# State-space layer between two batches: a new order of the work, other PSUM banks, tanh in place of silu in the gated MLP, and copies, skip terms and first scalings put on VectorE and GpSimd

## The reference

```python
def _mamba(h, in_proj_W, conv_w, conv_b, x_proj_W, dt_proj_W, dt_proj_b, A_log, Dp, out_proj_W):
    x, z = jnp.split(h @ in_proj_W, 2, axis=-1)          # 512 channels each
    x = _silu(causal_conv4(x, conv_w) + conv_b)          # 4 taps, per channel
    xdbl = x @ x_proj_W                                  # 16 + 32 + 32 columns
    dt = jax.nn.softplus(xdbl[..., :16] @ dt_proj_W + dt_proj_b)
    Bm, Cm = xdbl[..., 16:48], xdbl[..., 48:]
    A = -jnp.exp(A_log)
    # for every time step: hst = hst * exp(dt*A) + dt*B*x ;  y = sum_n hst * C
    _, ys = jax.lax.scan(step, h0, seq)
    y = ys + Dp * x                                      # the skip term
    return y * _silu(z) @ out_proj_W

h = _ln(x, norm1_w, norm1_b) * (1 + s1) + sh1
x = x + g1 * (_mamba(h) + flip(_mamba(flip(h))))
h = _ln(x, norm2_w, norm2_b) * (1 + s2) + sh2
x = x + g2 * (_silu(h @ w1) * (h @ w2) @ w3)
```

## Time and profile before

| | |
|---|---|
| median of 3 runs | 5845.14 us |
| profiled execution, its own time | 5844.69 us |
| its span | 5842.8 us |
| the fourth layer's pace | 8 batches of 128 units, one every 344.0 us |
| busy over the span: PE, DVE, ACT, POOL | 94%, 74%, 70%, 48% |
| instructions with a scan (L2480) | 1024, 2267 ns each |

### The profile page before, as it was taken

How to read it: one execution, slowest core, us unless ns; L and a number is a source line. 1 busy time by engine, 2 the same in 40 slices (tenths; PEclk the granted TensorE clock), 3 DMA queues, 4 the chain that set the end, 5 groups by cost and what they waited for, 6 DMA issues and landing times. The chain is left out here.

```text
span 5842.8 us, 74727 instructions
## 1 busy us (share of the span) xinstructions
PE 5511.4 (94%) x27336; PEld 2865.9 (49%) x27336; DVE 4311.1 (74%) x5020; ACT 4113.3 (70%) x6785; POOL 2804.3 (48%) x2191
## 2 busy tenths in 40 slices
PE   8999999999999997999998999999999999999998
PEld 5444445555555554444444444444544445454445
DVE  6767744444444444776867989899898999989898
ACT  3555454554444543555558989899998989989897
POOL 0000012232222321010106969699696978969697
PEclk8999999999999998999999999999999999999999
DMA  5342420000000004233223020110202012020200
GB/s 145 47 66 34 83 30 3 1 3 3 2 3 1 3 2 63 48 62 63 48 45 69 30 54 30 42 43 24 59 30 54 30 29 56 26 58 30 54 30 22
DMA packets 171934, 222.33 MB, mean 38 GB/s; under 512 B 40881, under 2 KB 107274, under 8 KB 171314
## 3 DMA queue, kind: packets, MB, share of 16 engines
q1 hardware_dynamic: 171570, 217.56, 17.1%
HBM read 152.90 MB, written 30.49 MB: 31 GB/s over the span
## 5 line engine op out<-in xcount | busy, mean ns | idle before, releaser
L2480 DVE TENSOR_TENSOR_SCAN l__h<-l__decay,psum 128x1024 f32<-128x1024 f32 x1024 | 2249.6, 2267 | 55.9 <-ACT l__decay L1928 15.5
L2446 POOL TENSOR_TENSOR l__hc<-l__h,l__c_rep 128x1024 f32<-128x1024 f32 x1016 | 2012.4, 2013 | 92.5 <-DMA l__c_rep<-l__c_dram 46.5
L1928 ACT ACTIVATE l__decay<-l__dt_rep,l__a_neg 128x511 f32<-128x511 f32 x2048 | 1339.6, 708 | 9.6 <-DVE l__h L2480 9.3
L1938 PEld LDWEIGHTS psum<-ident,l__dtx_B 128*128 128x128 f32 x8192 | 882.7, 141 | 850.9 <-DVE l__h L2480 496.1
L2564 PE MATMUL psum<-l__hc,l__gather 128*64 128x512 f32 x4096 | 1105.2, 618 | 139.8 <-POOL l__hc L2446 139.3
L1938 PE MATMUL psum<-ident,l__dtx_B 128*128 128x128 f32 x8192 | 1119.3, 280 | 35.6 <-DVE l__h L2480 16.8
L1912 ACT ACTIVATE l__dtx_B<-l__dtx_T,l__b_T 128x512 f32<-128x512 f32 x1664 | 1103.4, 709 | 5.5 <-PE psum L1938 3.4
L683 DVE TENSOR_REDUCE l__row_max<-psum 128x1 f32<-128x512 f32 x1024 | 648.7, 680 | 207.4 <-PE psum L717 203.8
L1367 POOL TENSOR_SCALAR l__probs<-l__probs,l__rec 128x512 f32<-128x512 f32 x512 | 348.6, 694 | 886.4 <-DVE l__rec L1363 886.4
L199 POOL TENSOR_SCALAR l__ln_var_eps<-l__ln_mean_var 128x4 f32<-128x4 f32 x56 | 16.1, 287 | 1433.6 <-DVE l__ln_mean_var L185 1433.6
L1040 ACT ACTIVATE l__probs<-psum 128x1024 f32<-128x1024 f32 x512 | 501.9, 1023 | 147.5 <-PE psum L1101 141.2
(11 more groups left out here) (184 smaller groups left out, 6193.9 us busy)
## 6 DMA issues: line engine op xcount, KB each, us to landing
l__c_rep<-l__c_dram SPq DMA_DIRECT2D x512, 128.0 KB, 2.8
l__dt_rep<-l__dt SPq DMA_DIRECT2D x128, 256.0 KB, 5.0
l__parts_dram<-l__parts SPq DMA_DIRECT2D x64, 384.0 KB, 3.5
l__q_stack<-l__parts_dram SPq DMA_DIRECT2D x192, 128.0 KB, 6.5
l__k_stack<-l__parts_dram SPq DMA_DIRECT2D x192, 128.0 KB, 9.1
l__w<-in_l_w SPq DMA_DIRECT2D x6, 1024.0 KB, 6.3
l__gate_rows<-l__gates_dram SPq DMA_DIRECT2D x24, 256.0 KB, 3.2
in_mod_w<-in_mod_w SPq DMA_DIRECT2D x1, 4608.0 KB, 17.8
```

The lines of the kernel that those rows point to most:

```text
L1928: nc.scalar.activation(decay[:, i % DECAYS, s, 1:T], dt_rep[:, w, c, s, 1:T], ACT.Exp, scale=a_neg[:, g, c, s:s + 1]).then_inc(S["decay"], 1)
L1938: last = nc.tensor.transpose(bx_psum(i)[:, s, t * P:(t + 1) * P], dtx_B[:, (k + 1) % 2, t, 2 * c + s, :, :].rearrange("p j d -> p (j d)"), ...
L2446: nc.gpsimd.tensor_tensor(hc[:, i % HCS, :, :], h[:, i % HS, :, :], c_of(i), ALU.mult).then_inc(S["hc"], 1)
L2480: nc.vector.tensor_tensor_scan(both(h[:, i % HS, :, :]), both(decay[:, i % DECAYS, :, :]), both(bx_psum(i)), 0.0, ALU.mult, ALU.add).then_ ...
```

## The change

- **VectorE.** The first chunk of the convolution comes between gates 1 and 2. The normalised rows (L193) follow the statistics at once. New on it are: the copy of the backward half of `dc`, the copy of the transposed B, the scaling and shift of the MLP's input out of PSUM (two), the four backward copies of dt*x transposed, four of the eight first scalings, and a second multiplication for each of the MLP's three products. The skip terms have gone.
- **GpSimd.** It makes the skip terms, eight instructions of 128 x 512 (`skip_terms`): xs forward + xs backward, then times D.
- **ScalarE.** Skip terms, half the copies, B's copy, the MLP's input and four scalings have gone; silu of x comes ahead of silu of z; the MLP uses tanh(u/2), from which VectorE makes u*(1 + tanh(u/2)) and then 0.5 times this times the second projection; the third tanh stands behind the first two units' decays.
- **TensorE.** The transposes of the next batch's layer norm come ahead of the last but two `y_sum`, the input projection begins in banks 0 and 1 between the last `y_sum`s, z's four projections come in one piece ahead of `project_x`, and the transposes of dt*x alternate between banks 4, 5 and 2, 3 in place of 0 and 1.
- **SyncE.** One wait for both halves of `dc` in place of two.

```diff
@@ -1843,9 +1845,10 @@
-        IN_BANKS = (2, 3, 0, 1)
+        IN_BANKS = (0, 1, 2, 3)
-        dt_banks = lambda c: psum[:, (2, 0, 4, 2)[c]:(2, 0, 4, 2)[c] + 2, :]
+        dt_banks = lambda c: psum[:, (0, 4, 2, 0)[c]:(0, 4, 2, 0)[c] + 2, :]
+        dtxT_bank = lambda c, w: bank[(4, 2)[c % 2] + w]
...
+        def scale_first(dve):
+            w, g, _ = split(0)
+            for op in range(VEC_OPS):
+                t, j = op // NJ, op % NJ
+                nc.vector.tensor_scalar(dtx_B[:, 1, t, :, j, :], dtx_T[:, w, t, :].rearrange("p (b d) -> p b d", d=HB),
+                                        b_T[:, w, t, NJ * g + j:NJ * g + j + 1], None,
+                                        ALU.mult).then_inc(S["dtxB_vec"], 1)
...
@@ between_gpsimd
+            if begin:
+                skip_terms(pool, end)
             if end:
                 norm.gpsimd(nc, pool, 1 if begin else 0)
...
+        def skip_terms(pool, end):
...
+            for c in range(IC):
+                pool.wait_ge(*S.at("xs", 2 * (c + 1)))
+                nc.gpsimd.tensor_tensor(y[:, c, :], xs[:, c, 0, :], xs[:, c, 1, ::-1], ALU.add).then_inc(S["y_first"], 1)
+                pool.wait_ge(*S.at("y_first", c + 1))
+                nc.gpsimd.tensor_scalar(y[:, c, :], y[:, c, :], dp[:, c:c + 1], 1.0, ALU.mult, ALU.mult)\
+                    .then_inc(S["y_init"], 1)
...
@@ between_vector
+            if begin and end:
+                gate(0)
+                gate(1)
+                convolve(dve, range(1))
+                gate(2)
+                gate(3)
+                convolve(dve, range(1, IC))
...
+                norm.stats(nc, dve, x_end, 1)
+                norm.scaled(nc, dve, x_end, 1)
+            dve.wait_ge(*S.at("dc_filled", 2))
+            nc.vector.tensor_copy(dc[:, 1, :], bank[DC_BANKS[1]][0:ROWS, :]).then_inc(S["dc"], 1)
+            dtx(0)
...
@@ between_scalar
-                take_x(act, IN_BANKS)
+                take_x(act, IN_BANKS, scanned=True)
...
+            silu_x(0)
+            silu_x(1)
+            silu_x(2)
+            silu_z(0)
+            silu_z(1)
+            silu_x(3)
+            silu_z(2)
+            silu_z(3)
+            act.wait_ge(*S.at("dc_filled", 1))
+            nc.scalar.activation(dc[:, 0, :], bank[DC_BANKS[0]][0:ROWS, :], ACT.Copy).then_inc(S["dc"], 1)
...
+                for j in range(HC - 1):
+                    tanh_up(j)
...
+            for i in range(DECAYED):
+                act.wait_ge(s_dt_rep[split(i)[2]], dt_rep_of(nxt))
+                decay_unit(i)
             if end:
+                tanh_up(HC - 1)
...
@@ tensor_batch
+                if i == UNITS - 1 and begin:
+                    pe.wait_ge(*S.at("scan", UNITS - 1))
+                    norm.tensor(nc, pe, 0, bank[0:DC])
                 if i >= 2:
                     y_sum(i - 2)
             if begin:
-                pe.wait_ge(*S.at("scan", UNITS - 1))
-                norm.tensor(nc, pe, 0, bank[0:DC])
+                pe.wait_ge(*S.at("hT", DC))
+                project_in(pe, 0)
             y_sum(UNITS - 2)
             if begin:
-                pe.wait_ge(*S.at("scan", UNITS))
-                pe.wait_ge(*S.at("hT", DC))
-                project_in(pe, 0)
+                project_in(pe, 1)
             y_sum(UNITS - 1)
             if begin:
-                project_in(pe, 1)
+                pe.wait_ge(*S.at("scan", UNITS))
                 project_in(pe, 2)
                 project_in(pe, 3)
```

More of the change, by code:

```diff
@@ L2326, in between_tensor @@
-            if end:
-                if begin:
-                    pe.wait_ge(*S.at("bT", 1))
-                norm.tensor(nc, pe, 1 if begin else 0, bank[6:8])
-            if begin:
-                fill_dtx_T(0)
+            for c in range(IC):
+                project_in(pe, IC + c)
+            for c in range(IC):
+                project_x(c)
+            project_dt(0)
+            project_dt(1)
+            for w in range(2):
+                for t in range(TT):
+                    last = nc.tensor.transpose(bT_psum[:, w, t * NS:(t + 1) * NS], dc[b_rows[w], w, t * P:(t + 1) * P],
+                                               ident[b_rows[w], b_rows[w]])
@@ L2332, in between_tensor @@
+            last.then_inc(S["bT_filled"], 1)
+            project_dt(2)
+            project_dt(3)
+            if end:
+                pe.wait_ge(*S.at("bT", 1))
+                norm.tensor(nc, pe, 1, bank[6:8])
+            fill_dtx_T(0)
+            fill_dtx_T(1)
             if end:
-                pe.wait_ge(*S.at("hT", (2 if begin else 1) * DC))
+                pe.wait_ge(*S.at("hT", 2 * DC))
                 project_up(0)
-            if begin:
-                for c in range(1, IC):
-                    fill_dtx_T(c)
@@ L2353, in between_tensor @@
-            if begin and not end:
-                pe.wait_ge(*S.at("dt", IC))
+            fill_dtx_T(2)
+            fill_dtx_T(3)
+            if not end:
                 for i in range(FILLED):
                     first_fill(i)
+                return
+            project_up(1)
+            project_up(2)
+            first_fill(0)
+            pe.wait_ge(*S.at("prod", HC))
+            first_fill(1)
+            for t in range(TT):
+                for j in range(HC):
+                    last = nc.tensor.matmul(bank[6 + t // 2][:, (t % 2) * D:(t % 2 + 1) * D],
+                                            hid[:, j, t * P:(t + 1) * P], w3[:, j, :],
+                                            start=(j == 0), stop=(j == HC - 1))
+                if t % 2:
+                    last.then_inc(S["down_filled"], 1)
```

224 lines of the change are left out of this document (86 added, 138 removed).

## The result

The changed kernel takes 5884.74 us (median of four runs, 5875.36 to 5887.85), the kernel before, run beside it, 5846.55 us (four runs, 5843.84 to 5849.3). The ratio is 1.0063, 95% interval 1.0048 to 1.0078: slower by some 38 us, where the prediction said 5883 in a range from 5842 to 5899. The profiled execution took 5887.85 us, with a span of 5886.0 us against 5842.8.

A forecast was written before the change was run, and what follows sets the result against it. TensorE bounds the transition. Per transition +5.1 (first dt projection) - 0.8 (then to third fill) + 1.7 (clock) = +6.0 us; seven make 42, less 1.5: +40.5 on 5844.69, so 5885, shaded to 5883; range 5842 to 5899.

The forecast's parts named there:

- the mechanism forecast with 0.62: GpSimd's skip terms stop VectorE's taps, `dc` copy and dt projection come late, TensorE's clock falls; +6.0 us per transition.
- the idle time of 6 us: Sign in the new profile: TensorE idles some 6 us before the dt projection, with the copy of `dc` as releaser.
- first mark without interference: Start of the first dt projection, if VectorE and GpSimd don't disturb each other: 4464.4, 0.4 us gained.
- interference at the first mark: With VectorE and GpSimd excluding each other, the first dt projection starts at 4469.9, 5.1 us later than before.
- between the marks at full clock: From first dt projection to the new batch's third fill on TensorE: 28.0 us for 28.77, 0.8 less.
- clock: TensorE's granted clock falls to half after its idle time before the dt projection: +1.7 us per transition.
- 3 x 1.96 = 5.9 us during which VectorE stands: Three GpSimd skip terms, 1.96 us each, fit before the last tap and stop VectorE, so taps end at 4459.8.
- rival 1: Taps keep GpSimd out until the last; first dt projection +2.8, +2.5 to +3.7 us per transition, 5861 to 5869; chance 0.14.
- Some 3.4 us of work at half speed cost 1.7 us: Price of TensorE's slow clock after idling, taken from the first batch's start in the earlier trace.
- Rival 4: Clock stays at half through the B and layer-norm transposes: another 2 us per transition, 5897; within the forecast's 0.62.
- the second fill's wait: TensorE's second fill waits for the MLP's last product: 0.54 us before, 1.3 us with the added multiplication.
- The first batch: The layer's first batch, with no MLP beside it, saves a table load and half the copies: 1.5 us taken.

The follow-up runs named there:

- e1: Changed kernel with VectorE's copy of `dc` put ahead of the normalised rows (L193): 5836.13 us, 0.9974 of the kernel before.
- e4: Changed kernel with GpSimd's eight skip-term instructions replaced by memsets of the same tiles: 5831.75 us, 0.9973 of the kernel before.
- e2: Changed kernel with twenty unread transposes on TensorE filling its wait for the `dc` copy: 5852.95 us, 1.0007 of the kernel before.
- e5: Changed kernel with one memset on VectorE between the taps of the second and third of the last three chunks: 5885.73 us, one run.
- e10: e9 with silu in place of tanh, all three ahead of the decays, one plain product each: 5828.37 us, 0.9971 of the kernel before.
- e9: e1 with five unread transposes on TensorE in its wait for the `dc` copy: 5830.1 us, and 5827.74 us in a second run.
- e3: Changed kernel with GpSimd's skip terms put behind the layer norm's two instructions: 5846.67 us, 0.9996 of the kernel before.
- e8: e1 with z's last two projections kept behind `project_x`, their silu behind the `dc` copy: 5838.98 us, 0.998 of the kernel before.

## Why the prediction was right, and where not

The time was right, and so was the sum per transition, but by luck: the mechanism forecast with 0.62 isn't the one that happened, and three of the four terms were wrong. The prediction's own test says so. It calls itself wrong if the eighteen taps still take 12 us and GpSimd's skip terms lie behind them, and both are in the profile. Of its other signs TensorE's idle time in front of the dt projection (2.87 us, with the copy of `dc` as releaser), the one dip of the clock, the earlier first tap (+4.17 for +6.03 us) and the one table load less (three for four) appeared; the idle time of 6 us and the taps of 1.9 us did not. Each step, in us per transition:

| step | forecast | measured |
|---|---|---|
| first mark without interference | -0.4 | -0.6 (e1, e4) |
| interference at the first mark | +5.5 | +2.1 (after against e1) |
| between the marks at full clock | -0.8 | -1.45 (27.31 in e1 and e2 against 28.77) |
| clock | +1.7 | +5.9 (periods of after and e2) |
| sum | +6.0 | +5.9 (41.5 over seven) |

- **Interference.** The place, the victim and the chain were right: skip terms beside taps, `rstd` late, VectorE's copy of `dc` behind L193, TensorE idle in front of the dt projection. The step that failed is "3 x 1.96 = 5.9 us during which VectorE stands". I gave each GpSimd instruction the port when it asks. The trace shows that the taps keep it: they take 12.00 us, GpSimd's first addition 7.38. That was rival 1, at 0.14. Its +2.8 at the first mark was nearer than my +5.1 to the +1.5 that came. About half of the 1.3 us that are left is `rstd`: I gave it the 2.2 us of before, but with VectorE standing idle its two instructions took 1.35 (0.23 and 1.04, from 4484.31 to 4485.66).
- **A row that I passed over.** The prediction says that nothing in the trace shows a GpSimd instruction that arrives second. The trace of before has one, in the transition of the rows:

```profile
4459.25 1.38 DVE L2109 SCALAR_TENSOR_TENSOR l__y<-l__xs,l__dp,l__y 128x512 f32<-128x512 f32 x2
4459.43 0.63 POOL L199 TENSOR_SCALAR l__ln_var_eps<-l__ln_mean_var 128x4 f32<-128x4 f32 x1 [25.47 <-DVE l__ln_mean_var L185]
4460.15 1.38 POOL L202 TENSOR_TENSOR l__ln_rstd<-l__ln_var_eps,minus_half 128x4 f32<-128x4 f32 x1
```

L199 starts during the first of VectorE's two skip terms, takes 0.63 us for 0.23 and ends at 4460.06, 0.09 us behind that first one; the second doesn't keep it out. L202 beside the second takes 1.38 for 1.04. That is where the 2.2 us of before come from, and it is taking turns, as in e5, for an instruction of 4 elements per partition. It wouldn't have told of the nine taps.
- **The clock.** The step that failed is "Some 3.4 us of work at half speed cost 1.7 us". I took from the earlier trace rows how much work fell into the slow stretch there, where TensorE had little to do, and even that was read wrong: the rows have 3.02 and 2.80 us of work at 0.50. They also tell nearly how long the lower level lasted, and the window between them completes it:

```profile
3114.00:3118.00 4.00, 0.48 (x3) 0.49 (x3) 2.83 (x2) 2.85 (x5) 0.00 (x0) 0.50 0.35 103
```

So it was 0.50 from 3110 to 3121, some 11 us. In the transition TensorE is fully busy behind its wait, so the price is half of such a stretch. In the windows of the new kernel the clock is down from 4488 to about 4498, and the marks lie 32.3 or 33.6 us apart for e2's 27.3. Rival 4 had the right direction, and +2 where +4.2 was needed.
- **The two errors** have opposite signs, -3.4 and +4.2, and nearly cancel. Rival 1 as I had priced it ends at 5869, 16 us short of the result; with its +2.8 and the clock's measured 5.9 it would have come to 5844.7 + 7 x 7.9 - 1.5 = 5898.5, 14 us too long.
- **Between the marks** the copies and the second fill's wait went as forecast (1.26 us for the 1.3 named). The tanh is a loss of 0.7 us and not nothing (e10). The gain is still larger than forecast: these 1.26 us are all of TensorE's idle time that is left there, and its busy time fell too, from the earlier trace rows's 26.73 to 26.05 us in e2, which I didn't foresee and didn't follow up.
- **The first batch** was to save 1.5 us. Measured from the start of the last down projections of the layers before it, its first scan comes at 54.1 us before and at 53.4 in the changed kernel, and its last product with C at the same time (339.7). But e2 and e5, which leave the first batch as the changed kernel has it, have 51.9 and 51.3, and the last product 1.7 and 1.6 us sooner than before; e1 and e9 are alike (51.2 to 51.4, and 1.5 to 1.9). So the forecast's 1.5 is borne out, and what the changed kernel's one profiled execution lost there isn't its code's; why it did stays open.

## What to carry to other kernels

Before a step is put behind another one in an engine's queue, ask which of the two somebody waits for: here a copy of 0.69 us that TensorE needed at once stood behind a scaling whose rows TensorE took up 8 us after they were done, and that one behind eight instructions on a third engine. Price a new wait of TensorE by what the granted clock does after it, and read that price from how long a slow stretch lasts in the profile, not from how much work it happened to hold there: a wait of 2.9 us cost 2.1 directly (against e1, which waits 0.8) and 5.9 by the clock. When two engines exclude each other, work out both outcomes, the other kept out until the queue ends (the changed kernel) and the two taking turns (e5), since both occur.

## What the runs showed of the hardware

- The granted clock fell to 0.50 behind 2.9 us of idle time in each of seven transitions and stayed there for 10 or 14 us of full work, in turn. With less idle time it fell in some transitions and not in others that have the same rows: with 0.78 us in one of fourteen (e1 and e4), with 0.93 and then 0.7 us in two of seven (e3), with 0.47 us behind small products in three of seven (e8). With 0.67 us behind twenty transposes (e2) and 0.23 behind five (e9, e10) it didn't fall in seven and in twenty-one.
- VectorE instructions with two inputs in SBUF, issued without a gap, drew out a GpSimd addition of 1.27 us to 7.38 us. One instruction without such inputs among them let it in, and from then on the engines took turns one by one (e5). GpSimd's memsets weren't held up (e4). The Trainium skill (SBUF — State Buffer, Who interferes with whom) calls the shared ports an exclusive lock and says, of VectorE's two-port modes, that whoever issues first blocks the other for the whole instruction. It speaks of single instructions; here the other waited for nine of them in a row.
- A tensor_scalar from SBUF to SBUF with one tile read, L193, was held up as well: 3.57 us for 1.39 beside GpSimd's skip terms (e3).
